# A fused layer on one core: no memset behind the indirect transfers that the plan issues beside the last tile

## The reference, cut to what matters

```python
x = x + 0.5 * ffn(layernorm(x), gate_w, w1, w3, w2)
x = x + attn(layernorm(x), ...)          # RWKV time mixing, a scan along the sequence
x = x + 0.5 * ffn(layernorm(x), gate_w, w1, w3, w2)

def ffn(x, gate_w, w1, w3, w2):          # 8 experts, the best two for each token
    probs = softmax(x @ gate_w)
    weights, experts = top_k(probs, 2);  weights /= weights.sum(-1)
    for i in range(8):
        wi = where(experts == i, weights, 0).sum(-1)
        out += (silu(x @ w1[i]) * (x @ w3[i])) @ w2[i] * wi[..., None]
```

## Time and profile before

| | us |
|---|---|
| median of 3 runs | 626.63 (625.92 to 626.74) |
| the profiled execution | 627.05 |
| its span | 625.2 |
| busy in the span: PE / PEld | 520.5 (83%) / 477.0 (76%) |
| busy in the span: DVE / ACT / POOL | 423.6 (68%) / 319.0 (51%) / 393.9 (63%) |
| L753, the 232 memsets of pace | 132.9 |
| L737, the 128 gathers | 125.0 |

### The profile page before, as it was taken

How to read it: one execution, slowest core, us unless ns; L and a number is a source line. 1 busy time by engine, 2 the same in 40 slices (tenths; PEclk the granted TensorE clock), 3 DMA queues, 4 the chain that set the end, 5 groups by cost and what they waited for, 6 DMA issues and landing times.

```text
span 625.2 us, 18560 instructions
## 1 busy us (share of the span) xinstructions
PE 520.5 (83%) x5866; PEld 477.0 (76%) x5866; DVE 423.6 (68%) x1218; ACT 319.0 (51%) x703; POOL 393.9 (63%) x499
## 2 busy tenths in 40 slices
PE   1235899999999999998999959998989999989910
PEld 1134789898888889788897759888889899978910
DVE  4862853556878898799998956878788674234421
ACT  5433664444585475855766524756464444434400
POOL 1171059499899960699819984005949878917983
PEclk9999899999999999999999979999999999989975
DMA  8963233544232222212221232111123343314322
GB/s 282 330 190 110 65 95 106 161 143 119 74 114 66 77 70 65 69 60 78 73 61 57 70 100 77 44 35 40 57 82 92 87 110 98 91 35 112 83 75 59
DMA packets 89062, 59.55 MB, mean 95 GB/s; under 512 B 10256, under 2 KB 82704, under 8 KB 88976
## 3 DMA queue, kind: packets, MB, share of 16 engines
q1 hardware_dynamic: 55296, 29.97, 16.4%
q0 software_dynamic: 8192, 16.79, 8.8%
q10 hardware_dynamic: 25488, 11.61, 6.4%
HBM read 28.65 MB, written 29.69 MB: 93 GB/s over the span
## 4 chain that ended last, share of the span: by engine, by line
PE 54%; POOL 11%; DVE 11%; ACT 11%; issue 8%; DMA 3%; POOLq 0%; ACTq 0%; DVEq 0%; SPq 0%
PE py L1258 17%; PE pa L1244 14%; PE pb L1244 12%; POOL yg L737 4%; POOL pace L753 3%; POOL rows_in L725 3%; ACT xn L816 3%; PE bkB L1317 2%; PE pT L1231 2%; PE bkB L1296 2%; DVE h L1113 2%; ACT sil L797 2%; PE bkA L1311 1%; PE bkA L1296 1%; DVE stats L903 1%
## 5 line engine op out<-in xcount | busy, mean ns | idle before, releaser
L725 POOL DMA_INDIRECT rows_in<-parts,slot x128 | 134.7, 1052 | 183.6 <-DVE slot L1038 161.7
L1113 DVE TENSOR_TENSOR h<-sil,pb 128x512 f32<-128x512 f32 x177 | 120.5, 685 | 127.4 <-ACT sil L797 77.9
L1258 PE MATMUL py<-ffn_w,h 128*128 x1416 | 197.8, 283 | 9.4 <-ACT yrow L782 9.0
L1258 PEld LDWEIGHTS py<-ffn_w,h 128*128 128x128 f32 x1416 | 174.7, 194 | 15.2 <-issue 12.3
L1244 PE MATMUL pa<-rT,ffn_w 128*128 128x128 f16 (+1 forms) x1752 | 151.1, 233 | 22.6 <-issue 12.6
L1244 PE MATMUL pb<-rT,ffn_w 128*128 128x128 f16 (+1 forms) x1752 | 155.2, 232 | 0.0
L1244 PEld LDWEIGHTS pa<-rT,ffn_w 128*128 x1752 | 123.9, 99 | 37.4 <-issue 25.9
L737 POOL DMA_INDIRECT yg<-rows_out,slot x128 | 125.0, 977 | 37.2 <-issue 21.2
L753 POOL MEMSET pace<- 128x544 uint8 x232 | 132.9, 573 | 0.2
L1244 PEld LDWEIGHTS pb<-rT,ffn_w 128*128 x1752 | 122.5, 98 | 7.0
L797 ACT ACTIVATE sil<-pa 128x512 f32<-128x512 f32 x177 | 105.3, 595 | 40.5 <-PE pa L1244 40.0
(11 more groups left out here) (156 smaller groups left out, 458.7 us busy)
## 6 DMA issues: line engine op xcount, KB each, us to landing
rows_out<-yrow ACTq DMA_DIRECT2D x177, 64.0 KB, 1.7
rin<-rows_in SPq DMA_DIRECT2D x65, 128.0 KB, 2.9
rows_in<-zrow SPq DMA_DIRECT2D x34, 128.0 KB, 2.1
shared<-in_w SPq DMA_DIRECT2D x16, 256.0 KB, 6.6
rin<-rows_in SPq DMA_DIRECT2D x47, 64.0 KB, 1.9
rows_in<-zrow SPq DMA_DIRECT2D x2, 1472.0 KB, 10.9
xres<-in_x SPq DMA_DIRECT2D x4, 512.0 KB, 6.4
ffn_w<-in_w SPq DMA_DIRECT2D x8, 256.0 KB, 5.2
```

Source lines behind the costliest of these rows:

```text
L725: pool.indirect_dma_start(rows_in[g][:], bass.IndirectOffsetOnAxis(ap=slot[:, c, at:at + 1], axis=0), parts[:, at, :], None).then_inc(s_sc ...
L1113: dve.tensor_tensor(h[:, t % RING, :], sil[:, t % 2, :], pb[t % 2][:], ALU.mult).then_inc(s_h, 1)
L1258: mm = pe.matmul(py[:], h[:, step % RING, at:at + T], w, start=(c == 0), stop=(c == FC - 1))
```

## The change

The memset and the wait on s_pace ahead of it are issued only where the transfer's tile number is below TILES - 1 = 176. Nothing else differs.

```diff
-            for sent, (_, name, *one) in enumerate(TRANSFERS):
+            for sent, (t, name, *one) in enumerate(TRANSFERS):
                 if name == "scatter":
                     scatter(*one)
                 else:
                     gather(*one)
-                wait(pool, s_pace, sent - PACES + 1)
-                pool.memset(pace[:, sent % PACES, :], 0).then_inc(s_pace, 1)
+                if t < TILES - 1:
+                    wait(pool, s_pace, sent - PACES + 1)
+                    pool.memset(pace[:, sent % PACES, :], 0).then_inc(s_pace, 1)
```

## The result

| set of runs | the kernel before, us | the changed kernel, us (lowest to highest) | ratio (95% interval) |
|---|---|---|---|
| first (the result) | 626.32 | 622.05 (620.04 to 623.24) | 0.9929 (0.9914 to 0.9943) |
| second, chip 2 | 628.98 | 632.51 (629.59 to 633.78) | 1.0072 (1.0048 to 1.0096) |
| third, chip 8 | 629.17 | 633.24 (631.70 to 634.12) | 1.0065 (1.0046 to 1.0083) |
| fifth, chip 13 | 626.29 | 622.61 (621.27 to 622.89) | 0.9943 (0.9928 to 0.9959) |

The fourth and the sixth set, on chips 9 and 2, held other kernels. The ratios leave out one execution of the kernel before, of the second set, that ran slow throughout (1549 us at a granted clock of 0.36).

A forecast was written before the change was run, and what follows sets the result against it. The prediction took POOL's serial stream to bound the tail: nine steps falling from 15.22 to 11.39 us save 3.83, giving 622.8 us from the median of 626.63. Its own range was 622.2 to 623.5, the wide one 622.0 to 624.6.

The forecast's parts named there:

- The steps of POOL: GpSimd's last nine spaced gathers: 1.68 us a step with memset, 1.25 without; nine steps save 3.83 us.
- one long gather too many: Gather burst at the end: one gather 0.11 us longer kept among the nine steps, another in the seven steps behind.
- the forecast's own range: Whole kernel: 622.2 to 623.5 us, for long gathers, the shared-input rule and spread of runs; chance 0.80.
- the wide one: Whole kernel: the range 622.0 to 624.6 us, taking in the forecast and most of the first rival.
- The wait on s_pace: Ahead of the nine memsets: passed by the sequencer while POOL works, so it costs nothing of its own.
- The closing drain as a constant behind the last gather: POOL's end: the drain releases the program 9.2 us after the last gather ended and moves with it.
- the third rival: POOL's closing drain grows with the number of unspaced gathers, 10.4 us more, less 3.83: 633.2 us; chance of slower 0.05.
- The company of the burst: Unspaced gathers beside last matmuls, stores and combine: a gather may be slower than 1.25 us; price seen 0.11, one of two.
- The cover of 1.7 us ahead of the stores: First gather behind the wait for the stores: possible from about 600.4, wanted at 602.1; later stores would take gain.
- the first rival: Longer burst of 17 gathers: slower gathers or late stores lose part of the gain, 624.8 us; chance 0.08.
- the other side: Whole kernel: the outcome that the change makes it slower, argued only through a growing closing drain; chance 0.05.
- that rule: Gathers beside VectorE's two-input combine: each of two could wait one 0.29 us instruction, making the gain 3.4 us, time 623.3.

The follow-up runs named there:

- again3: The changed kernel run once more, unaltered, in the fifth set on chip 13; 622.61 us, 0.9943 of the kernel before.
- nowait: Kernel before with all memsets; the last nine write to scratch columns of their own, without the wait on s_pace ahead of them; 628.47 us, ratio 1.0002.
- drainlate: Changed kernel, with GpSimd also waiting behind its last gather, ahead of its closing drain, until the last block is combined; 624.92 us, 0.9979 of the kernel before.
- fenced: Changed kernel, with GpSimd waiting ahead of the first of the nine unspaced gathers until TensorE's last down product is done; 632.39 us, 1.0054 of the kernel before.
- last4: Kernel before without the memsets of the last four planned transfers, in place of nine; 627.15 us, ratio 0.9989.

## Why the prediction was right or wrong

**The steps of POOL: right.** 1.68 us with a memset and 1.25 without, in every trace. The sum kept one long gather too many in each part of the burst: 4.11 us came off between the first unspaced step and the last gather, where 3.83 were forecast. The start of the burst, at 591.02 in place of 590.70, took 0.3 back, and the profiled execution's span fell by 3.8. By the medians the gain was 4.3 us, the forecast 3.83, the interval of the ratio 3.6 to 5.4. The time, 622.05, lies 0.15 us below the forecast's own range (622.2 to 623.5) and only 0.05 above the lower end of the wide one. Of the 0.75 us under the forecast 0.31 come from where the sum began, at 626.63, while the kernel before ran at 626.32 beside it. The rest comes from two of the six runs (spans of 618.2 and 618.4 at a mean clock of 0.976, the four others 620.0 to 621.4 at 0.970 to 0.971): the four alone have a median of 622.5, a gain of 3.8. `again3` is scattered too (621.27 to 622.89) and gains 3.7 us. What makes these runs quicker was not settled. (One aside of the prediction is off and touches no sum: whoever subtracts the memset's 0.57 in place of 0.43 counts a third too much, not a quarter.)

**The wait on s_pace: right**, shown by `nowait`. **The closing drain as a constant behind the last gather: right**: it ends 9.2 to 9.3 us behind that gather's end in the traces of all kernels but `drainlate`, which shows that the constant is the drain's own length; the third rival, a drain that grows, is out: it took as long after 17 unspaced gathers as after 8.

**The company of the burst: wrong, and here the prediction failed.** The step read: a gather without a memset between it and the next may be slower in company, and the price seen is 0.11 for one of two. That asked what TensorE, VectorE and the stores do to the gathers. It never asked what the gathers do to TensorE, and so put that term at nothing. In the second and third set unspaced gathers make TensorE's down products known late, three in a row by 2.1, 2.6 and 1.8 us behind their modelled ends in the third set and the first by 3.5 us in the second, so that they are issued up to 5.2 us apart in place of 1.6; with a step of 1.68 us they are on time in the same sets. The measured price is 7.6 us of waiting for the last store, less the 3.8 to 4.1 us saved: the 3.5 and 4.1 us of loss. That the first result came out near the forecast was the luck of the set: it was of the kind in which this term is nothing.

**The cover of 1.7 us ahead of the stores: right as worked out** (the waits were passed by 600.4 and the gather ran at 602.27, although the last stores took 1.9 us to land in place of 1.5), and right in what it would cost if the stores came later. But the first rival named only the DMA engines that gathers and stores share as what could make them late, with 1 us for each 1 us and a chance of 0.08. The mechanism that did it, TensorE held up, stood in no rival, and the other side was given 0.05.

**Could the trace of before have shown it?** Not its size: that execution was of the kind without stops, and its announcements show no gap. What it did show was a program that spends 132.9 us of POOL's time on memsets nobody reads, beside TensorE at 83%. The question what those memsets keep apart was open, and only more runs could answer it.

**The Trainium skill.** Its page SBUF — State Buffer, section Who interferes with whom, knows one meeting point between GpSimd and another engine, the ports it shares with VectorE. The forecast weighed that rule at 0.58 us; in the changed kernel the gathers beside the combine at 593.55 took 0.94, so it didn't show. The same section says that a DMA never contends with a compute engine. In the second and third set indirect transfers held up TensorE, and `fenced` freed it. That the contact is at SBUF isn't shown, but whoever takes the sentence to mean that transfers leave TensorE's timing alone is contradicted there, and the measurement decides.

## What to carry to other kernels

A filler instruction that nobody reads is a question to the trace: ask not only what it costs its own engine, but what its neighbours would meet without it. When indirect transfers run beside matmuls, keep their spacing until the last matmul is out, and drop it behind it; that part (`last4`) did no harm even where TensorE was stopped, though its interval doesn't tell its gain from none. And time a change of 1% in more than one set of runs: here four sets each had an interval clear of no change, two on either side. Where semaphore records are missing from a trace, read a delay from the engine that waits and not from the records.

## What the runs showed of the hardware that was not expected

- In two of six sets of runs indirect transfers make results of TensorE known late, by up to 0.8 us when spaced, with semaphore records of all engines missing from about 0.7 to 1.2 us behind a transfer's start; in the other four sets they do neither. The kernel before is some 3 us slower in the former. Chip 2 showed both kinds. What sets the kind was not found, nor which part of a transfer does it, nor whether TensorE's work or only the word of it is held.
- The same gathers, 1.46 us apart, cost TensorE little (down products 1.6 to 2.4 us apart). Nine unspaced ones, 1.25 us apart, put the products up to 5.2 us apart, and beside thirteen the matmuls themselves went out one each 0.7 us.
- GpSimd's closing drain took 9.21 us once its queue was empty, and it bound the end here, where GpSimd's gathers are the last long chain.
